# The inverse y transform of a Fourier layer in four 32-row tiles instead of two 64-row tiles, with the 1x1 convolution ahead of it

## The reference, cut to what matters

```python
x_ft = jnp.fft.rfft2(v)                                   # v: batch, channel, x, y
out1 = jnp.einsum('bixy,ioxy->boxy', x_ft[:, :, :M1, :M2], W1)   # 12 x 12 modes
out2 = jnp.einsum('bixy,ioxy->boxy', x_ft[:, :, -M1:, :M2], W2)
...
x1 = jnp.fft.irfft2(out_ft, s=(Sx, Sy))
x2 = jnp.einsum('bcxy,cd->bdxy', v, w_w[i]) + w_b[i][None, :, None, None]
v = x1 + x2                                               # then batch norm, and ReLU in layers 0 to 2
```

## Time and profile before

| | us |
|---|---|
| median of 3 runs | 1064.14 (1061.94 to 1066.07) |
| profiled execution | 1064.5 |
| its span | 1062.6 |
| TensorE matmuls busy / weight loads busy | 717.9 / 521.6 |
| VectorE busy | 677.5 |
| ScalarE busy | 383.2 |
| GpSimd busy | 65.5 |
| mean granted TensorE clock over the span | 0.835 of 2.4 GHz |

### The profile page before, as it was taken

How to read it: one execution, slowest core, us unless ns; L and a number is a source line. 1 busy time by engine, 2 the same in 40 slices (tenths; PEclk the granted TensorE clock), 3 DMA queues, 4 the chain that set the end, 5 groups by cost and what they waited for, 6 DMA issues and landing times. The chain is left out here.

```text
span 1062.6 us, 26488 instructions
## 1 busy us (share of the span) xinstructions
PE 717.9 (68%) x12228; PEld 521.6 (49%) x12228; DVE 677.5 (64%) x1011; ACT 383.2 (36%) x478; POOL 65.5 (6%) x93
## 2 busy tenths in 40 slices
PE   3559937677993777897476799651765756776781
PEld 2447723366771336676133677411554655655450
DVE  6827669945777983577797378602647466364558
ACT  0014459002456600345740044341345543535421
POOL 2500000020000002000001000001020100100000
PEclk9969869978996996999699699785786886878695
DMA  8420000050000004000003000012000010000000
GB/s 234 95 45 3 2 2 1 2 181 2 3 3 1 2 29 153 2 3 3 1 1 120 4 3 3 2 16 79 1 8 17 1 70 1 1 0 1 1 1 20
DMA packets 13983, 29.62 MB, mean 28 GB/s; under 512 B 5456, under 2 KB 5840, under 8 KB 13712
## 3 DMA queue, kind: packets, MB, share of 16 engines
q1 hardware_dynamic: 13872, 27.92, 9.0%
HBM read 26.87 MB, written 1.05 MB: 26 GB/s over the span
## 5 line engine op out<-in xcount | busy, mean ns | idle before, releaser
L330 ACT ACTIVATE V<-ps,wts 128x1024 f32<-128x1024 f32 x128 | 135.7, 1112 | 408.7 <-PE ps L571 408.7
L435 DVE BATCH_NORM_STATS2 stats<-V 128x6 f32<-128x512 f32 x256 | 157.2, 678 | 65.4 <-ACT V L330 65.4
L571 PE MATMUL ps<-tab,A 64*128 64x128 f32 x2048 | 146.2, 291 | 41.8 <-ACT V L330 20.2
L571 PEld LDWEIGHTS ps<-tab,A 64*128 64x128 f32 x2048 | 128.2, 196 | 74.7 <-issue 41.8
L390 DVE STREAM_TRANSPOSE A<-V 128x2048 f32<-128x2048 f32 x48 | 107.4, 2278 | 6.7 <-ACT V L324 6.7
L429 DVE STREAM_TRANSPOSE A<-ps 128x2048 f32<-128x2048 f32 x32 | 73.9, 2314 | 53.7 <-PE ps L556 51.4
L517 PE MATMUL ps<-A,tab 128*128 128x384 f32 x192 | 71.7, 519 | 39.4 <-DVE A L397 39.4
L324 ACT ACTIVATE V<-V,small 128x2048 f32<-128x2048 f32 x48 | 95.7, 2084 | 5.0 <-DVE small L468 5.0
L505 PE MATMUL ps<-A,tab 32*32 32x512 f32 x1536 | 61.1, 654 | 37.8 <-DVE A L390 37.8
L1108 PE MATMUL tps<-cst,nrm 128*128 128x128 f32 x72 | 20.9, 448 | 89.7 <-DVE nrm L967 89.7
L517 PEld LDWEIGHTS ps<-A,tab 128*128 128x128 f32 x192 | 35.9, 197 | 84.6 <-DVE A L397 67.6
(11 more groups left out here) (153 smaller groups left out, 986.5 us busy)
## 6 DMA issues: line engine op xcount, KB each, us to landing
A<-in_modes SPq DMA_DIRECT2D x32, 384.0 KB, 7.6
r_ky<-in_modes SPq DMA_DIRECT2D x16, 384.0 KB, 6.1
wl<-in_layers SPq DMA_DIRECT2D x4, 643.0 KB, 4.2
V<-in_grid SPq DMA_DIRECT2D x12, 120.0 KB
wm<-in_mixture SPq DMA_DIRECT2D x1, 1162.0 KB, 6.5
tab<-in_table SPq DMA_DIRECT2D x1, 656.5 KB, 5.0
A<-in_turned SPq DMA_DIRECT2D x1, 512.0 KB, 4.3
tower_out<-A SPq DMA_DIRECT2D x4, 128.0 KB
```

The source lines that it names most:

```text
L330: nc.scalar.activation(Vm[:, 2 * h:2 * h + 2, r, 512 * q:512 * (q + 1)], bank(half_of_u(q, r) + 2 * h, 2).rearrange("p (m n) -> p m n", m= ...
L435: last = nc.vector.bn_stats(stats[:, 16 * q + 4 * r + m, :], Vm[:, m, r, 512 * q:512 * (q + 1)])
L571: last = nc.tensor.matmul(ps[:, at:at + P], G[(2 * q + quad) % 4][rows, x:x + P], inv_y[rows, :], start=step < 2 and quad == 0, stop=step ...
```

## The change

The inverse y transform is cut into tiles of 32 rows. Each holds one batch, so the moving operand is 64 columns wide and has no zeros. Four tiles, one for each 32-row group, are issued together and write four different banks; over the four steps each row group visits each bank. A unit has 32 such matmuls instead of 16. The convolution goes first, as 16 matmuls of 512 columns instead of 32 of 256, and it starts the accumulation (`start=True`). Between the four steps TensorE waits for its own last matmul of the step before, three times in a unit instead of once. The order of units, of inverse_x and of all other engines' work stays.

```diff
--- before.py
+++ after.py
@@ -562,31 +562,32 @@
                     kernel, depth = (conv_w[l], Q) if l else (lift_w, 4)
 
                     def inverse_y(step):
+
                         for quad in range(2):
-                            for h in range(2):
-                                rows = slice(64 * h, 64 * (h + 1))
-                                i = (step + 2 * h) % 4
+                            for n in range(4):
+                                rows = slice(Q * n, Q * (n + 1))
+                                i = (step + n) % 4
                                 x = Q * (16 * i + 4 * r)
-                                at = 512 * (base + i) + 256 * quad + P * h
-                                last = nc.tensor.matmul(ps[:, at:at + P], G[(2 * q + quad) % 4][rows, x:x + P], inv_y[rows, :],
-                                                        start=step < 2 and quad == 0, stop=step >= 2 and quad == 1,
-                                                        tile_position=(64 * h, 0))
+                                at = 512 * (base + i) + 256 * quad + S * n
+                                last = nc.tensor.matmul(ps[:, at:at + S], G[(2 * q + quad) % 4][rows, x:x + P],
+                                                        inv_y[rows, S * (n % 2):S * (n % 2 + 1)],
+                                                        start=False, stop=step == 3 and quad == 1, tile_position=(Q * n, 0))
                         return last
 
-
-
-                    inverse_y(0)
+                    for j in range(4):
+                        for i in range(4):
+                            rows = slice(Q * i, Q * i + depth)
+                            nc.tensor.matmul(bank(base + i)[Q * j:Q * (j + 1), :], kernel[rows, :],
+                                             Vm[rows, j, r, 512 * q:512 * (q + 1)], start=True, stop=False,
+                                             tile_position=(Q * i, Q * j))
+
+                    turns = 3 * (UNITS * l + 4 * q + r)
+                    inverse_y(0).then_inc(s_half, 1)
+                    pe.wait_ge(s_half, turns + 1)
                     inverse_y(1).then_inc(s_half, 1)
-                    for half in range(2):
-                        for j in range(4):
-                            for i in range(4):
-                                rows = slice(Q * i, Q * i + depth)
-                                out = bank(base + i)[Q * j:Q * (j + 1), :].rearrange("p (s h n) -> p h s n", s=2, h=2)[:, half]
-                                src = Vm[rows, j, r, 512 * q:512 * (q + 1)].rearrange("p (s h n) -> p h s n", s=2, h=2)[:, half]
-                                nc.tensor.matmul(out, kernel[rows, :], src, start=False, stop=False,
-                                                 tile_position=(Q * i, Q * j))
-                    pe.wait_ge(s_half, UNITS * l + 4 * q + r + 1)
-                    inverse_y(2)
+                    pe.wait_ge(s_half, turns + 2)
+                    inverse_y(2).then_inc(s_half, 1)
+                    pe.wait_ge(s_half, turns + 3)
                     inverse_y(3).then_inc(s_U, 1)
```

## The result

The changed kernel takes 1146.43 us (median of 4 runs, 1142.58 to 1152.48) against 1065.11 us for the kernel before in the same comparison: a ratio of 1.0773, interval 1.0719 to 1.0827. The forecast was 1129 us. The profiled execution is the one of 1142.58 us, the shortest of the four, with a span of 1140.7 us.

The account below looks back on a forecast made before the run. The chain of TensorE's units and ScalarE's eviction was taken to bound the stage; +35 us in layer 0 and +30 in layers 1 to 3 on 1064.5 gave 1129 us. Range 1082 to 1185, the forecast's own 1110 to 1155.

Parts of the forecast that it names:

- Bound: Inverse y stage: convolution units A and B on TensorE, 7.14 us, then ScalarE's eviction of B, 2.17 us, make the cycle.
- Rounds at 0.112: Inverse y transform: each of 16 rounds of four matmuls takes 0.112 us, as each pair did before, despite half the moving columns.
- Rival 3: Inverse y rounds go at the pace of streaming, 0.056 us, so a step takes 0.51 and the kernel 1035 us; chance 0.07.
- Three waits at 0.735 us a step: Between a unit's four inverse y steps: 0.41 to the last record, 0.275 for that record, 0.05 until TensorE starts again.
- Convolution 1.11: Start of each unit: convolution of 512-column matmuls takes 1.11 us to the next load instead of 1.42, a gain of 0.31.
- Cycle 10.14: Stage at 2.4 GHz: 3.93 + 4.04 + 2.17 us per cycle, was 9.31; five cycles per layer add 4.15 us.
- Stage of layers 1 and 2: Inverse y stage of layers 1 to 3: 73.3 us before, expected 10 us longer in each, 30 for three.
- Step and unit at 1.2 GHz: Inverse y stage at the lower clock: a step takes 1.23 us, a unit 6.7 us.
- The clock falls in layer 0 and mostly holds elsewhere: Layer 0 mostly at 1.2 GHz, its stage 113 us (+35); layers 1 to 3 mostly at 2.4 GHz.
- Rival 1: Clock holds in all layers after its first rise, so the change costs 27 us, 1092 us in all; chance 0.16.
- Rival 2: Clock stays low for most of the stage in layers 1 to 3 too: +151 us, 1216 in all; chance 0.14.
- a third of the next unit at 1.2 GHz: Start of the stage in layers 1 to 3: after the first inverse_x, slow clock adds 0.9 us per layer.

Follow-up runs that it names:

- e6: Changed kernel with each inverse y matmul loading 64 of the 128 stationary columns, so half of the transform's output is left out: 1060.0 us, ratio 0.9983.
- e5: Changed kernel, waits kept, with 128 instead of 64 moving columns in each 32-row tile, the table's zeros streamed too: 1148.3 us, ratio 1.0716.
- e1: Changed kernel without the three waits, each row group writing one bank in all steps, so sums stand in wrong banks: 1074.5 us, ratio 1.0097.
- e2: Kernel before with only the convolution put first as 16 matmuls of 512 columns, 64-row tiles and one wait kept: 1062.0 us, ratio 0.9986.
- e4: Changed kernel with layer 0's convolution contracting over 32 rows instead of 4, on other weights and data: 1105.4 us, ratio 1.0412.
- e7: Changed kernel with the convolution contracting over 4 rows in all four layers, not in layer 0 alone: 1223.8 us, ratio 1.1534.
- e9: Changed kernel without the three waits, sums in wrong banks, and with 128 instead of 64 moving columns per 32-row tile: 1035.8 us, ratio 0.9743.

## Why the prediction came out as it did

The direction, the mechanism and the size were right; the median is 17 us above the forecast and inside the forecast's own range. Step by step:

1. Bound (TensorE's units and ScalarE's eviction in one chain): right. VectorE and ScalarE kept their busy times and waited longer.
2. Rounds at 0.112 because of the loads, so that halving the moving columns gains nothing: right, shown by e6 (half the stationary columns, a step 0.21 shorter) and by e5 (twice the moving columns, a step 0.05 longer). Rival 3 rested on the opposite and is out.
3. Three waits at 0.735 us a step: 0.76, as TensorE waits 0.086 us past its own record's end rather than 0.05. e1 gives the price of all three by itself, 0.95 us per unit. One reading in this sum was wrong: the first matmul's record was put 0.054 us after its load. No row shows that. The changed kernel's first records start within 0.01 us of their loads, and the second round's 0.16 later instead of 0.11, so the last record of a step starts at 0.41 as forecast.
4. Convolution 1.11: 1.09. e2 shows that the gain is what one uncovered wait costs.
5. Cycle 10.14: 10.25. Stage of layers 1 and 2 expected 83.3 (73.3 + 10): 83.2 and 83.3. That it agrees to 0.1 us is luck. In layer 1 five cycles cost 4.7 us more than before instead of 4.15, and the last five units 2.6 instead of 2.4, while what the stage's start and the stretch at 1.2 GHz add came to 2.6 instead of 3.4. Step and unit at 1.2 GHz 1.23 and 6.7: 1.22 and 6.66.
6. The clock falls in layer 0 and mostly holds elsewhere: right; layer 0 116.8 against 113. e4 and e7 show that the convolution's rows decide between 85 and 117 us. Rival 1 (1092 us) rested on gaps between bursts; e4 and e7 have the same matmul shapes in columns, the same waits and order and differ in rows (and in the data of those rows), so gaps alone don't decide. e1 says so too: with the three waits gone, matmul records cover 103.7 of layer 0's 105.9 us and the clock is still 0.52. Rival 2 did not occur where the convolution is full; e7 shows what it would have been, 1224 us (I had put 1216).

Where it was off, in the profiled execution (1142.6, not 1129.5): layer 0 +3.8, the rest of the kernel +2.2, and layer 3 +7.2. In layer 3 the step that failed is "a third of the next unit at 1.2 GHz": there the clock came up late. Its stretches, behind one of layer 1:

```profile
299.60:371.00 71.40, 63.33 (x1560) 42.81 (x1528) 49.58 (x66) 30.29 (x29) 0.00 (x0) 1.00 0.01 3
664.80:675.00 10.20, 9.94 (x152) 6.69 (x120) 1.43 (x1) 2.12 (x2) 0.00 (x0) 0.50 0.01 2
675.00:678.40 3.40, 3.17 (x96) 2.46 (x96) 3.24 (x5) 0.12 (x1) 0.00 (x0) 1.00 0.00 0
678.40:688.60 10.20, 9.94 (x152) 6.69 (x120) 3.38 (x5) 4.12 (x4) 0.00 (x0) 0.50 0.01 2
...
702.40:753.00 50.60, 45.22 (x1128) 30.40 (x1096) 34.98 (x48) 21.56 (x21) 0.00 (x0) 1.00 0.01 3
```

It rose at 675, fell again at 678.4, and held only from 702.4, 38 us after the stage's start; in layer 1 it held from 299.6, 10 us after the start. The program is the same in both. I did not find what makes the difference within one kernel, nor did I trace the executions that took up to 1152 us. The executions of one kernel do go with their mean granted clock: 0.785 in the one of 1142.6 us and 0.775 in the one of 1152.5, and for e5 0.814 in the one of 1133.3 and 0.794 in the one of 1156.9. What stays open is why one execution's stage warms early and another's late. Also open is e5's layer 0: why more streaming with the waits in place was no help, and whether its zeros count for less. e9 shows only that 128 columns without waits are enough in layer 0 (0.94).

## What to carry to other kernels

Before cutting a matmul into more and smaller row tiles, look whether its rounds are set by the moving columns or by the load of the stationary ones: a group with a short moving operand in the same trace tells it (0.11 us for 64 columns as for 128). If it is the load, smaller tiles save nothing and only bring the waits that keep the row groups out of one another's banks, each of which cost 0.32 us here, where nothing independent stood in front of it. And compute the cost at both clock levels: a stage in which the granted clock already fell at times before the change (here the layer with 4-row tiles) can lose more by the clock than by all added waits.

## What the runs showed of the hardware that I had not expected

- TensorE waiting on its own matmul starts 0.086 us after the record's end; ScalarE started 0.05 us after one.
- Doing more can be quicker: 28 more rows in layer 0's convolution took 32 us off its stage (e4), twice the moving columns without waits 37.6 us (e1 to e9).
- The Trainium skill ("TensorEngine Tiling (Array Packing)", Theoretical Speedup) allows up to 4x for 32 rows and up to 2x for 64. Here four 32-row tiles gave no more than two 64-row tiles: 16 rounds of four in 1.88 us (e1), 16 pairs in 1.86.
